# Weights and projected values of the later stages split into high and low parts inside the batch loop; second product of the expert layer turned round

## What is computed

```python
x = x + xattn(ctx_1024, layernorm(x), mask)   # 16 heads of 64; keys: 1601 context rows + 64 latents
x = x + attn(layernorm(x))                    # causal, 16 heads of 16, rotary q and k, W_o, b_o
x = x + ffn(layernorm(x))                     # 4 experts, the best 2 of 4 chosen by a router
# ffn, xf = rows x 256, H = 1024:
gates = softmax(top_k(xf @ wr + br, 2))
h = gelu(xf @ w1[e] + b1[e]);  y = h @ w2[e] + b2[e]
c = gelu(b1[e]) @ w2[e] + b2[e];  c_sum = sum over e of c[e]
out = sum over the 2 chosen e of gate * (y[e] - c[e] + c_sum)
```

## Time and profile before

| | |
|---|---|
| median of three runs | 2032.33 us |
| the profiled execution | 2036.69 us |
| its span, first to last instruction | 2034.9 us |
| PE busy | 1900.8 us (93%) |
| PEld busy | 1672.0 us |
| DVE / ACT / POOL busy | 1347.6 / 948.4 / 618.6 us |
| mean granted clock of PE | 0.966 |

### The profile page before, as it was taken

One profiled execution on the slowest core, in us unless ns is written; L12 is line 12 of the kernel. 1 busy time (PEld: TensorE's weight loads), 2 busy tenths in 40 slices (PEclk: granted clock), 3 DMA queues, 4 the chain that ended last, 5 costly groups with the idle time before them and its releaser, 6 DMA issues. The chain is left out here.

```text
span 2034.9 us, 33329 instructions
## 1 busy us (share of the span) xinstructions
PE 1900.8 (93%) x10868; PEld 1672.0 (82%) x10868; DVE 1347.6 (66%) x3077; ACT 948.4 (47%) x1616; POOL 618.6 (30%) x661
## 2 busy tenths in 40 slices
PE   6889999999999999999999999999999868869998
PEld 4678888888888888888888888888888756648887
DVE  6576767777676767676767777676766358745555
ACT  4544545454545454545545454545454322234443
POOL 3332315050404042332415050404140067611110
PEclk9899999999999999999999999999999978769999
DMA  8620201010111112020201011111111030011100
GB/s 279 229 59 16 51 27 41 26 40 27 41 37 30 39 40 50 15 50 15 50 26 40 26 40 39 30 36 30 47 19 40 3 125 22 1 52 42 43 21 21
DMA packets 111097, 94.94 MB, mean 47 GB/s; under 512 B 70720, under 2 KB 92608, under 8 KB 111040
## 3 DMA queue, kind: packets, MB, share of 16 engines
q1 hardware_dynamic: 111040, 94.19, 16.2%
HBM read 71.11 MB, written 23.07 MB: 46 GB/s over the span
## 5 line engine op out<-in xcount | busy, mean ns | idle before, releaser
L222 PE MATMUL o_bank<-probT,val 128*128 128x512 f32 x2496 | 684.9, 410 | 7.3 <-DVE probT L831 5.0
L222 PE MATMUL s_bank<-keyT,qkT 128*128 128x416 f32 x3072 | 627.5, 355 | 0.7 <-DVE qkT L836 0.7
L222 PEld LDWEIGHTS s_bank<-keyT,qkT 128*128 128x128 f32 x3072 | 573.8, 189 | 22.1 <-DVE qkT L836 1.3
L222 PEld LDWEIGHTS o_bank<-probT,val 128*128 128x128 f32 x2496 | 438.9, 189 | 90.1 <-DVE probT L831 11.6
L796 ACT ACTIVATE prob<-prob,negmax 128x1665 f32<-128x1665 f32 x128 | 216.2, 1689 | 381.3 <-DVE negmax L860 381.3
L831 DVE TENSOR_TENSOR probT<-t_bank,probT 128x512 fp32r<-128x512 f32 x416 | 283.1, 687 | 147.5 <-ACT probT L774 143.0
L774 ACT ACTIVATE probT<-t_bank 128x512 fp32r<-128x512 f32 x416 | 242.4, 590 | 232.9 <-PE t_bank L923 231.6
L855 DVE CUSTOM_DVE_ANT_0 prob<-s_bank,bias 128x416 f32<-128x416 f32 x512 | 296.1, 586 | 81.4 <-PE s_bank L222 80.4
L923 PE MATMUL t_bank<-ident,prob 128*128 128x128 f32 x1664 | 251.0, 274 | 11.0 <-DVE probT L831 7.0
L923 PEld LDWEIGHTS t_bank<-ident,prob 128*128 128x128 f32 x1664 | 205.5, 140 | 53.3 <-DVE probT L831 14.4
L337 POOL TENSOR_TENSOR small<-stats 128x9 f32<-128x9 f32 (+1 forms) x32 | 6.7, 210 | 706.8 <-DVE stats L303 706.8
(11 more groups left out here) (187 smaller groups left out, 1972.1 us busy)
## 6 DMA issues: line engine op xcount, KB each, us to landing
stage<-in_ctx SPq DMA_DIRECT2D x48, 512.0 KB, 3.6
qk_scratch<-qk_stage SPq DMA_DIRECT2D x32, 512.0 KB, 4.0
qk<-qk_scratch SPq DMA_DIRECT2D x16, 1024.0 KB, 6.8
y_scratch<-ystage SPq DMA_DIRECT2D x32, 128.0 KB, 1.7
yraw<-y_scratch SPq DMA_DIRECT2D x8, 512.0 KB, 3.8
stage<-in_w SPq DMA_DIRECT2D x4, 1024.0 KB, 4.8
w2raw<-in_w SPq DMA_DIRECT2D x4, 1024.0 KB, 5.7
mask<-in_mask SPq DMA_DIRECT2D x16, 200.1 KB, 6.6
```

The source lines that it names most:

```text
L222: mm = pe.matmul(out, weights(a), moving(b), start=first and n == 0, stop=last and n == 2)
```

## The change

Four parts.

1. **The splits of the weights move into the batch loop.** The host packs all weights of the later blocks into `wall`, 16 slices of 128 x 1280. A new event W at chunk 4 of X splits one slice per batch: SP loads it (640 KB), ACT copies the high part, POOL subtracts for the low part, SP stores both (1280 KB) into `w_scratch`. Blocks 2 and 3 load weights that are split already, which is twice the bytes.
2. **The projected values are split where they are made.** Event Y does two ACT copies and two DVE subtractions of 64 x 256 in place of one copy on each, and SP stores a high and a low part in pieces of 256 bytes. Block 2 loads them in pieces of 512 bytes and splits nothing.
3. **Loads.** The loads of `wout`, `wqk` and `wvs` at the end of the loop are gone; block 2 loads its own weights, and `w1`, `w2` and the small tensors of block 3.
4. **The expert layer.** The second product has `w2` as weights and `hT` as the moving side, 512 columns a matmul, and sums all four experts in four PSUM banks. The gate is applied to the hidden values by DVE, as (h - gelu(b1)) x gate in place in `hid`, which now has 8 slots; for that the gates are laid out along the rows (by eight small matmuls for expert 0, through memory for the others). The `gbs` product is replaced by 16 DVE passes per expert into `cacc` and one matmul at the end. The sum is transposed back and added to `x2`.

Core of the diff ("..." where lines are left out):

```diff
+X_AT = {"W": 4, "P3": 10, "Y0": 1, "N0": 3, "N1": 7, "S4": 6, "S0": 10, "S1": 12}
+            if c == X_AT["W"] and has_a:
+                ev += [("W",)]
...
-            if b.off == B:
-                sp.wait_ge(val_done, 4 * B)
-                for n, (name, at, k, width) in enumerate(STAGED):
-                    sp.dma_start(staged(W["stage"], at, k, width), ...).then_inc(W["self_in"][n], 16)
+                wait(pool, w_high, b, 1, 1)
+                pool.tensor_tensor(w_split[:, 1, :], w_raw[:, :], w_split[:, 0, :].bitcast(F32), ALU.subtract
+                                   ).then_inc(w_low, 1)
...
+                    act.activation(ystage[0:L, e[1], 0, :, :], cols[0:L, :, 0, :], ACT.Copy)
+                    act.activation(ystage[L:P, e[1], 0, :, :], cols[L:P, :, 1, :], ACT.Copy).then_inc(t_high, 1)
+                if kind == "W":
+                    wait(act, w_raw_in, b, 16, 16)
+                    wait(act, w_out, b, 16, 0)
+                    act.activation(w_split[:, 0, :], w_raw[:, :], ACT.Copy).then_inc(w_high, 1)
...
         load_y(0)
+        sp.wait_ge(W["w_out"], 16 * B)
+        load_split(wout, WCOLS["wout"][0], w_in[0])
+        sp.dma_start(xin[:, :, :], ...)
         load_y(1)
+        for n, name in ((1, "wqk"), (2, "wvs")):
+            load_split(weights[n], WCOLS[name][0], w_in[n])
         ... (the seven constants)
+        load_split(wo, WCOLS["wos"][0], w_in[3])
+        load_split(E["w1"], W1_AT[0], W["w1_in"])
+        load_split(E["w2"], W2_AT[0], W["w2_in"])
...
+        def project(e, half, k):
+            for t in range(HT):
+                if k == 0:
+                    wait(pe, h_done, e, 16, 8 * half + t + 1)
+                mm = split_pair(pe, ybank[half][k][:, :], lambda q: w2[:, t, q, k * P:(k + 1) * P],
+                                lambda q: hT[:, t, q, HALF[half]], e.off == 0 and t == 0, ...)
...
+        for e in experts:                                  # ACT
+            lag = HRING - 1 if e.off == 0 else 3
+            def gelu(m):
+                wait(act, h_full, e, 16, m + 1)
+                wait(act, h_done, e, 16, m + 1 - HRING)
+                act.activation(hid[:, z, :], hbank[m % 2][:, :], ACT.Gelu, bias=b1[:, e.off, t:t + 1]).then_inc(h_gelu, 1)
+            def high(m):
+                wait(act, h_gated, e, 16, m + 1)
+                act.activation(hT[:, t, 0, HALF[half]], hid[:, m % HRING, :], ACT.Copy).then_inc(h_high, 1)
...
+                dve.scalar_tensor_tensor(out=cacc[:, :], in0=w2[:, t, q, :].bitcast(F32), scalar=gb[:, e.off, t:t + 1],
+                                         in1=cacc[:, :], op0=ALU.mult, op1=ALU.add).then_inc(c_step, 1)
...
+                    if e.off == E4 - 1 and (half, k) == (0, 1):
+                        pe.wait_ge(c_step, 2 * HT * E4)
+                        pe.matmul(rbank[0][:, 0:D], ones[:, :], cacc[:, :], start=True, stop=True).then_inc(c_full, 1)
+        pool.wait_ge(c_done, 1)
+        pool.tensor_tensor(x2[:, :, :], x2[:, :, :], csum[:, :].unsqueeze(1).to_broadcast([P, RT, D]), ALU.add
+                           ).then_inc(x2_plus, 1)
```

More of the change, by code:

```diff
@@ L50 @@
 QK_RING = 4
+WCOLS = {"wout": (0, PAIRS, D), "wqk": (2048, KD, 2 * D), "wvs": (3072, KD, D), "wos": (3584, KD, D)}
+W1_AT, W2_AT = [4096 + 4096 * e for e in range(E4)], [6144 + 4096 * e for e in range(E4)]
+WALL = 4096 + 4096 * E4
+WPART = WALL // B
+HRING = 8
+YRING = 2
+GATE_AT = (6, 7)
 HL3 = ((0, 0), (0, 1), (1, 0))
@@ L385, in prepare, with block_0 @@
             self.centre(pool, n, g)
-def block_0(nc, ins, F, W, ctx):
+def block_0(nc, ins, F, W, used, ctx):
     def sb(name, shape, dt):
@@ L641, in _, with block_1 @@
         tiles(gemm, absorb, lambda n: None)
[L645 to L652, removed]
+def block_1(nc, ins, F, y_scratch, w_scratch, shared, used, ctx):
     W = shared
@@ L1119, in __call__ @@
             self.eng.wait_ge(self.sem, self.n)
-    weights = [(staged(W["stage"], *where), to) for (_, *where), to in zip(STAGED, (wout, wqk, wv))] + [(wtmp, wo)]
+    weights = [wout, wqk, wv, wo]
     block = ctx.enter_context(nc.Block())
@@ L1596, in link @@
+        dve.wait_ge(logit_done, 1)
+        chain = [0]
         def link(ins):
@@ L1670, in _ @@
+        dve.wait_ge(sum_ready, 2)
+        dve.wait_ge(c_full, 1)
+        dve.tensor_tensor(csum[:, :], csum[:, :], rbank[0][:, 0:D], ALU.add).then_inc(c_done, 1)
+        dve.wait_ge(x2_plus, 1)
+        for t in range(RT):
+            dve.wait_ge(f_full, t + 1)
+            dve.tensor_tensor(x2[:, t, :], x2[:, t, :], rbank[(t + 1) % 2][:, 0:D], ALU.add).then_inc(fin_done, 1)
     @block.gpsimd
@@ L1730, in _, with hidden @@
-        experts(pe, body)
-def build(nc, ins, out, lat_scratch, qk_scratch, y_scratch):
+        def hidden(e, m):
+            half, t = divmod(m, HT)
+            wait(pe, h_gelu, e, 16, m - 1)
+            for k in range(KD):
+                mm = split_pair(pe, hbank[m % 2][:, :], lambda q: w1[:, k, q, t * P:(t + 1) * P],
+                                lambda q: xn2T[:, k, q, HALF[half]], k == 0, k == KD - 1)
+            mm.then_inc(h_full, 1)
+        def project(e, half, k):
[3 more added lines that the diff above has]
+                mm = split_pair(pe, ybank[half][k][:, :], lambda q: w2[:, t, q, k * P:(k + 1) * P],
+                                lambda q: hT[:, t, q, HALF[half]], e.off == 0 and t == 0, e.off == E4 - 1 and t == HT - 1)
+            mm.then_inc(y_full, 1)
@@ L1734, in build @@
+        for t in range(4, RT):
+            give_back(t)
+def build(nc, ins, out, lat_scratch, qk_scratch, y_scratch, w_scratch, gate_scratch):
     with ExitStack() as ctx:
@@ L1771 @@
     parts = np.arange(P)
+    w1, w2 = flat("L0_ffn_w1"), flat("L0_ffn_w2")
+    split = [flat("L0_xattn_Wout"), np.concatenate([flat("L0_attn_W_q")[order], flat("L0_attn_W_k")[order]], 0).T,
+             flat("L0_attn_W_v").T, flat("L0_attn_W_o").T, *(w[e] for e in range(E4) for w in (w1, w2))]
     arrays = {
```

514 lines of the change are left out of this document (243 added, 271 removed).

## The result

The changed kernel took 2039.23 us in the median of 7 runs (2037.59 to 2041.31), the kernel before 2027.37 on the same chip. The ratio on record is 1.0042, with a 95% interval of 1.0027 to 1.0058 (it is not the quotient of these two medians, which is 1.0058); a second measurement, in the experiments, gave 1.0027 (1.0013 to 1.0041). By these two ratios the change makes the kernel about 0.3 to 0.4% slower. I had forecast a gain: 2026 us against the median of 2032.33 that I had, and 2030.7 for the profiled execution, which took 2041.31.

What follows compares the result with a forecast made beforehand. PE, 98% busy, was taken to bound the batch loop, and a PE, ACT and DVE chain block 2. Loop +4, its end and block 2's head +14.5, block 3 -24.4: -6, so 2030.7 us profiled, 2026 against the median; range 2011 to 2041.

Steps and rivals of the forecast that it cites:

- (a): Batch loop: event W and the new Y, mostly covered, cost 0.17 us per batch; +4 us in all, bounds 0 and +20.
- the edge: End of the batch loop: the last Y ends one ACT copy, one DVE subtraction and a store issue later, +1.2 us.
- rival C: Batch loop: W's copy and subtraction make PE wait 1.3 us per batch, +22 there; total +12, 2044 us; chance 0.11.
- (b): End of the batch loop: last Y finishes later, +1.2 us; together with the head of block 2 +14.5, bounds +8 and +20.
- (c): Head of block 2: 7.5 MB of loads up to `vmask` take 24.1 us, so `vmask` lands 13.9 us later.
- +2.0 and -1.3: Block 2: tile 2's values 2.0 us late; about 1.3 us of waiting for POOL's `wqk` split at the head saved.
- (d): Block 3, the expert layer: 201.2 us against 225.6, -24.4 us, bounds -31 and -19.
- the ring: Expert 0's first product, tiles 8 to 15: gelu, high and low part run in series, about 2.1 us per tile against 1.37.
- lower clock after the ring: Start of expert 0's second product: PE at a lower clock there, 1.5 us.
- Rival B: Everything covered: loop pays nothing, loads run at 400 GB/s for +9, block 3 gives 26; total -17, 2015 us; chance 0.27.
- Rival D: Expert 0: PE's clock falls, +3.7 us over eight tiles and +1.5 at the second product; total -1, 2031 us; chance 0.12.
- band of under 0.5% either way: Whole kernel: time within 0.5% of before, chance 0.50, beside 0.38 for faster and 0.12 for slower.

Runs made afterwards that it cites:

- e_act_only: Changed kernel with event W's POOL subtraction cut to 8 of 1280 columns, ACT's copy full; loop ended at 1628.9 us, span at 2027.1 us, one run.
- e_pool_only: Changed kernel with event W's ACT copy cut to 8 of 1280 columns, POOL's subtraction full; loop ended at 1630.0 us, span at 2022.2 us, one run.
- e_head2: Changed kernel with block 2's seven constants loaded earlier and `w1`, `w2` and block 3's small tensors behind tile 3's values; 2022.22 us, single run.
- after: First profile of the changed kernel, unmodified; its span ended at 2039.5 us.
- r_after: The changed kernel, unmodified, measured and profiled a second time; 2038.65 us median of 12 runs, ratio 1.0027 to the kernel before.
- r_before: The kernel before, unmodified, executed once for a second profile; its span ended at 2030.9 us.
- e_pieces: Kernel before with POOL's subtraction for `w2`'s low part in eight instructions instead of one, all computed; 2011.39 us median of 5 runs, ratio 0.9896.
- e_before_short_low: Kernel before with POOL's subtraction for `w2`'s low part cut to an eighth, most low parts left out; 2005.02 us, single run.
- e_w_pieces: Changed kernel with event W in its old place and its POOL subtraction in five instructions instead of one; span ended at 2021.8 us, one run.

## Why the prediction was wrong, step by step

**(a), the loop, is the step that failed.** I took 0.17 us per batch and measured 0.75; with the edge I had +5.2 for the end of the loop and it was +12.7. That alone turns the sign: with +5.2 there, the span would have been 2.9 us shorter instead of 4.6 longer. The mechanism was on the page: the ACT copy ahead of transposed chunks and the stretched scaling are in (a) and in rival C. I weighed it by a row in which a stretched L867 left PE untouched, and in that row PE's next matmuls don't depend on the delay. I also misread the row: the POOL pass of 3.09 us beside it starts 2.03 us after L867; what ran when L867 started was the pass before it, 2.39 us from 904.12. The cost arises 15 us later, through the maximum and the exponential; and it arises only because two delays add up beyond what DVE's idle time absorbs, as e_act_only and e_pool_only show. A row with one of the two could not tell that. Rival C, with a chance of 0.11, had the source, event W, and the sign, but not the place where PE waits. Its price of 1.3 us a batch was almost twice too high: of 2.2 us of delay on DVE, 0.75 reached PE. Its total of 2044 is nearer to the 2039 measured than my 2026.

**(b) and (c), the head of block 2.** I had 24 us from the first load to `vmask` and measured 27.1; the bytes were right, the rate was taken too high (370 GB/s for the weights, where 304 to 352 were moved). I took the 400 GB/s of one window for what a whole queue of mixed pieces would reach. The page of the Trainium skill that I had set aside there, "DMA: Bandwidth & Descriptors", Specifications, says about 358 GB/s; of the four windows above, all are under it. Shorter slices behind them, at 1670 us, reached 426 GB/s, so here the figure is no ceiling. I also called tile 2's values 2.0 us late. They were: PE stands 1.56 us before the product at 1685.73, and in e_head2, where the values come earlier, this wait is gone. Tile 3 is late with it. From tile 1's first DVE pass to tile 3's it is 32.2 us in after and in r_after, and 28.3 in r_before, e_pieces, e_before_short_low and e_head2: 3.9 us, where my terms of +2.0 and -1.3 gave 0.6 in sum. Block 2 as a whole came to +18.5 against +13.3. The size was off here and not the mechanism: 3.0 for the rate and 3.3 for tiles 2 and 3, less about 1 elsewhere.

**(d), block 3, was right in nearly every term.** First tile 6.9 us after the block's start (6.8 forecast); expert 0's first product 29.3 (29.5), with the ring's period at 2.03 (2.1) and a PE wait of 1.6 for the gates' exponential (1.8); second product 22.0 (21.8); experts 1 and 2 43.8 each (43.7); the wait before the matmul on `cacc` 1.7 (2.3); expert 3 to the end 53.2 (54.2). Sum 199.0 against 201.2. Only the 1.5 us for a lower clock after the ring did not come. What I had not seen is how little of it the turned product would bring in the end: on b3 the whole change takes off 23.6 us, the short subtraction alone 22.5 and e_pieces 24.1.

**The others.** Rival B fell with the loop and the loads. Rival D fell: the second product of expert 0 ran at full speed, 22.0 us, behind a ring with waits of 0.37. Its price was misread too: 5.30 us for 12 matmuls are 2.65 for six, not 2.56. The range of 2011 to 2041 held the time, near its upper end, and the measured +0.3 to 0.4% lies in the band of under 0.5% either way that I gave 0.50. The sign was wrong. The range held because it was 30 us wide: the loop and block 2 came out 7.5 and 5.2 us slower than forecast, block 3 only 2.2 us faster.

## What to carry to other kernels

A delay put into a pipelined loop is not to be judged by the instruction behind it: follow the late engine through its chain to the next place where PE has no slack, and add up all delays that fall into the same stretch before comparing them with the idle time there. When a long POOL instruction stretches DVE's, cut it in pieces before rebuilding the algorithm; here that cost POOL 84% more time for the subtraction and gave the kernel 1%. And a queue of loads is an order of needs: what releases the first instruction and what the third tile needs go ahead of what is needed 150 us later; moving only the constants gave nothing here, since the third tile's values then set the time.

## What the runs showed of the hardware

- Cutting one POOL subtraction into eight made it slower by itself (4.57 to 8.41 us in a row with DVE's work between) and DVE's share of the wait smaller by far (4.88 to 1.03 us). The 1.03 us say that DVE gets its turn between two POOL instructions, also when the next one is queued. The Trainium skill, "SBUF — State Buffer", section "SBUF: two separate sides", says that the port pair which DVE and GpSimd share is held for the whole instruction; both e_pieces (4.88 to 1.03) and e_w_pieces (2.11 to 1.28) agree.
- PE's clock in block 2 took two courses for the same instructions: a stretch of 10 us at 0.50 in the profile of after and at 0.93 in that of r_after, worth 3.9 us in one tile. Five of the fourteen profiles have such a tile, in the kernel before and in the changed one. What decides between them was not found.
- A queue of mixed loads, most of their bytes in pieces of 512 bytes and more, ran at 304 to 352 GB/s over 24 us, where the kernel before had windows of 374 and 400.
